# A second layer norm and expert router moved from their own stage into a tile pipeline of attention

## The reference

```python
a   = layer_norm(c, ln1_w, ln1_b); a = conv1d(a, conv_w)          # causal, 3 taps
q, k, v = split(a @ attn_w); q, k = rotary(q), rotary(k)
y   = softmax(causal(q @ k.T / sqrt(16))) @ v                       # 16 heads of 16, sequences of 64
s   = c + y @ proj_w
h   = layer_norm(s, ln2_w, ln2_b)                                   # the second norm
idx = argmax(h @ router_w)                                          # 4 experts, the first of equals
out = x1 + s + sum_e where(idx == e, swiglu_e(h), 0)                # x1: the output of the first block
```

## Time and profile before

| | us |
|---|---|
| median of three runs | 2254.34 (2252.97 to 2255.35) |
| the profiled execution, its own time | 2255.13 |
| span of its profile | 2253.3 |
| tile pipeline, first TensorE work to last add | 1876.75 to 1975.19 |
| `layer_norm` stage, to the first matmul of the sort | 1976.07 to 2017.59 |
| first matmul of the experts | 2040.73 |

### The profile page before, as it was taken

How to read it: one execution, slowest core, us unless ns; L and a number is a source line. 1 busy time by engine, 2 the same in 40 slices (tenths; PEclk the granted TensorE clock), 3 DMA queues, 4 the chain that set the end, 5 groups by cost and what they waited for, 6 DMA issues and landing times. The chain is left out here.

```text
span 2253.3 us, 32388 instructions
## 1 busy us (share of the span) xinstructions
PE 2053.0 (91%) x11764; PEld 1725.6 (77%) x11764; DVE 1120.4 (50%) x1969; ACT 941.9 (42%) x1879; POOL 666.2 (30%) x713
## 2 busy tenths in 40 slices
PE   7999999999999999999998666899899666868998
PEld 6888888888888888888886455688799455747998
DVE  3333443434344344434435785423477566756775
ACT  4242323323232332424224697322355354555664
POOL 3030200203030120303100396110388143308884
PEclk9999999999999999999999698899899878978999
DMA  4010010101001010200001200410156123246661
GB/s 160 1 57 1 1 56 0 56 0 56 0 11 45 0 56 0 81 0 0 1 1 38 53 36 31 149 38 10 53 198 195 41 44 109 78 142 206 212 215 57
DMA packets 93436, 139.98 MB, mean 62 GB/s; under 512 B 15438, under 2 KB 70384, under 8 KB 93360
## 3 DMA queue, kind: packets, MB, share of 16 engines
q1 hardware_dynamic: 86304, 122.97, 17.1%
q0 software_dynamic: 4928, 12.86, 1.6%
q10 hardware_dynamic: 2128, 3.15, 0.4%
HBM read 106.96 MB, written 12.06 MB: 53 GB/s over the span
## 5 line engine op out<-in xcount | busy, mean ns | idle before, releaser
L584 DVE TENSOR_TENSOR cond_h<-cond_silu,ps 128x512 f32<-128x512 f32 x288 | 197.9, 687 | 697.6 <-ACT cond_silu L495 694.1
L495 ACT ACTIVATE cond_silu<-ps 128x512 f32<-128x512 f32 x288 | 172.3, 598 | 772.6 <-PE ps L414 772.6
L414 PE MATMUL ps<-a_x_hi,cond_w_hi 128*128 128x512 f32 x1152 | 449.8, 390 | 2.0 <-DVE a_x_lo L262 2.0
L414 PE MATMUL ps<-a_x_lo,cond_w_hi 128*128 128x512 f32 x1152 | 449.3, 390 | 0.0
L414 PE MATMUL ps<-a_x_hi,cond_w_lo 128*128 128x512 f32 x1152 | 449.1, 390 | 0.0
L383 POOL TENSOR_TENSOR cond_w_lo<-cond_stage_up,cond_w_hi 128x256 fp32r<-128x256 f32 x144 | 108.6, 771 | 833.7 <-ACT cond_w_hi L476 833.7
L414 PEld LDWEIGHTS ps<-a_x_hi,cond_w_hi 128*128 128x128 f32 x1152 | 216.9, 188 | 47.5 <-DVE a_x_lo L262 2.4
L414 PEld LDWEIGHTS ps<-a_x_hi,cond_w_lo 128*128 128x128 f32 x1152 | 216.9, 188 | 45.3
L414 PEld LDWEIGHTS ps<-a_x_lo,cond_w_hi 128*128 128x128 f32 x1152 | 216.9, 188 | 45.0
L430 PE MATMUL ps<-cond_h_hi,cond_d_hi 128*128 128x512 f32 x576 | 224.4, 390 | 3.4 <-DVE cond_h_lo L552 3.4
L430 PE MATMUL ps<-cond_h_hi,cond_d_lo 128*128 128x512 f32 x576 | 224.1, 389 | 0.0
(11 more groups left out here) (371 smaller groups left out, 4086.4 us busy)
## 6 DMA issues: line engine op xcount, KB each, us to landing
moe_stage_up<-in_L_ffn_expert_wv SPq DMA_DIRECT2D x22, 1024.0 KB, 8.4
typed_stage_up<-in_L_cond_wi SPq DMA_DIRECT2D x11, 1024.0 KB, 4.9
typed_stage_dn<-in_L_cond_wo SPq DMA_DIRECT2D x11, 1024.0 KB
moe_stage_dn<-in_L_ffn_expert_proj SPq DMA_DIRECT2D x11, 1024.0 KB
cond_stage_up<-in_L_cond_Wg SPq DMA_DIRECT2D x7, 1024.0 KB, 4.8
cond_stage_up<-in_L_cond_Wu SPq DMA_DIRECT2D x7, 1024.0 KB, 6.8
cond_stage_dn<-in_L_cond_Wd SPq DMA_DIRECT2D x7, 1024.0 KB, 5.1
hyp_v_now<-hyp_v_blk SPq DMA_DIRECT2D x16, 272.0 KB, 2.3
```

Of the source, the lines that this page charges most:

```text
L414: ins = pe.matmul(up_ps[st % 2][j], w[:, j, k, fs], x[:, k, tok], start=(i == 0), stop=(i == 3 * KC - 1))
L495: act.activation(silu[:, st % 2], up_ps[st % 2][0], ACT.Silu).then_inc(act_done, 1)
L584: dve.tensor_tensor(h[:, st % 2], silu[:, st % 2], up_ps[st % 2][1], ALU.mult).then_inc(up_free, 1)
```

## The change

`layer_norm` and its block are gone. The tile pipeline of the rotary attention has ten further phases, with tokens on the partitions:

- `out` now multiplies so that tokens are on the partitions (two matmuls 256 columns wide), and adds c by two matmuls of `router.res` (that tile's chunk of `m.sumT`, copied by SyncE) with the identity into the same bank. `add` is gone.
- `bring_sum` (SyncE, lag 4): two DMAs per tile, `router.res`, and `router.x` (the tile's rows of x1, from `typed_table` in HBM, where they already are).
- `stats`, `aggr` (VectorE), `rstd` (ScalarE, two small activations), `norm`, `total` (VectorE, read `out`'s bank), `weigh` (GpSimd, times ln2_w and plus ln2_b, rows), `store` (SyncE, one DMA per tile of h and total rows into `moe_table`).
- `h_turn` (TensorE, lag 6), `h_take` (ScalarE), `route` (TensorE), `keep` (VectorE, copies the logits). After the last tile `choose` picks the experts for all tiles at once, in nine small VectorE instructions.
- `y_take`, `out` have lag 5 instead of 4, the last lag is 6 instead of 4.
- hT_ps shares bank 0 with q's transposes, the logits bank 1 with k's, and y's transposes share bank 7 with `out`, which `norm` and `total` read; the added waits keep them apart.
- The weights of slot 0 are loaded at the head of the sort block (`SortFirst.sync`).

```diff
-            lag = dict(bring=0, turn=1, q_blk=1, k_blk=1, score=1, clamp=2, top=2, shift=2, prob=2, p_turn=3, p_take=3,
-                       mix=3, y=3, y_turn=4, y_take=4, out=4, add=4, fetch=1)
-            order = dict(tensor="y_turn p_turn out turn mix score", scalar="y_take p_take q_blk prob",
-                         vector="clamp top add k_blk y", gpsimd="shift", sync="bring fetch")
+            lag = dict(bring=0, turn=1, q_blk=1, k_blk=1, score=1, clamp=2, top=2, shift=2, prob=2, p_turn=3, p_take=3,
+                       mix=3, y=3, y_turn=4, y_take=5, out=5, fetch=1, bring_sum=4, stats=5, aggr=5, rstd=5, norm=5, total=5,
+                       weigh=5, h_turn=6, h_take=6, route=6, keep=6, store=6)
+            order = dict(tensor="out p_turn h_turn turn mix score route y_turn",
+                         scalar="y_take p_take h_take q_blk rstd prob",
+                         vector="clamp top stats k_blk aggr y norm total keep", gpsimd="shift weigh",
+                         sync="bring fetch bring_sum store")
...
+                    def bring_sum(i, q, nth):
+
+                        wait(sp, out_done, i - 1)
+                        sp.dma_start(router.res[:, q], resT[:, :, bass.ds(i * P, P)]).then_inc(sum_brought[q], 16)
+                        wait(sp, added, i - 1)
+                        sp.dma_start(router.x[:, q], router.x_rows[bass.ds(i * P, P)]).then_inc(sum_brought[q], 16)
+
+                    def store(i, q, nth):
+
+                        sp.wait_ge(weighed, i + 1)
+                        sp.wait_ge(added, i + 1)
+                        sp.dma_start(router.table[bass.ds(i * P, P)], router.rows[:, q]).then_inc(stored[q], 16)
+
+                    if not hyper:
+                        router.load(sp)
...
                         wait(pe, k_blocked, i)
+                        if not hyper:
+                            wait(pe, kept, i - 5)
...
                         wait(pe, q_taken, i)
+                        if not hyper:
+                            wait(pe, h_taken, i - 4)
...
                         wait(pe, y_taken, i)
                         wait(pe, added, i)
+                        if not hyper:
+                            wait(pe, normed, i)
...
                     def out(i, q, nth):
                         pe.wait_ge(y_taken, i + 1)
                         wait(pe, added, i)
+                        if not hyper:
+                            wait(pe, normed, i)
+                            pe.wait_ge(sum_brought[q], 32 * (nth + 1))
+                            for k in range(KC):
+                                pe.matmul(o_ps, yT[:, q, k], wo[:, k], start=(k == 0), stop=False)
+                            for c in range(KC):
+                                ins = pe.matmul(o_ps[:, c * P:(c + 1) * P], router.res[:, q, c], m.ident, start=False, stop=(c == KC - 1))
+                            ins.then_inc(out_done, 1)
+                            return
...
+                    def total(i, q, nth):
+
+                        dve.wait_ge(sum_brought[q], 32 * (nth + 1))
+                        wait(dve, stored[q], 16 * nth)
+                        dve.tensor_tensor(router.rows[:, q, D:], o_ps, router.x[:, q], ALU.add).then_inc(added, 1)
...
+                    def weigh(i, q, nth):
+
+                        pool.wait_ge(normed, i + 1)
+                        wait(pool, stored[q], 16 * nth)
+                        wait(pool, h_turned, i - 1)
+                        pool.tensor_tensor(router.xn[:, q], router.xn[:, q], router.w[:], ALU.mult).then_inc(scaled, 1)
+                        pool.wait_ge(scaled, i + 1)
+                        pool.tensor_tensor(router.rows[:, q, 0:D], router.xn[:, q], router.b[:], ALU.add).then_inc(weighed, 1)
...
     def sync(self, sp):
+        self.slots.load_slot(sp, 0, 0)
         sp.wait_ge(self.lists.owned, 1)
```

More of the change, by code:

```diff
@@ L1062, in bring @@
                         sp.dma_start(x[:, q], qk[:, bass.ds(i, 1)].rearrange("p o n -> p (o n)")).then_inc(brought[q], 16)
-                    run(sp, "sync", dict(bring=bring, fetch=fetch))
+                    def bring_sum(i, q, nth):
[9 more added lines that the diff above has]
+                        router.load(sp)
+                    run(sp, "sync", dict(bring=bring, fetch=fetch, bring_sum=bring_sum, store=store))
                 @block.tensor
@@ L1141, in out, with h_turn, route @@
                         ins.then_inc(out_done, 1)
-                    run(pe, "tensor", dict(turn=turn, score=score, p_turn=p_turn, mix=mix, y_turn=y_turn, out=out))
+                    def h_turn(i, q, nth):
+                        pe.wait_ge(weighed, i + 1)
+                        wait(pe, h_taken, i)
+                        wait(pe, q_taken, i + 5 if not isinstance(i, int) else min(i + 5, NP))
+                        for c in range(KC):
+                            ins = pe.transpose(hT_ps[:, c * P:(c + 1) * P], router.rows[:, q, c * P:(c + 1) * P], m.ident)
+                        ins.then_inc(h_turned, 1)
+                    def route(i, q, nth):
+                        pe.wait_ge(h_taken, i + 1)
+                        wait(pe, kept, i)
+                        wait(pe, k_blocked, i + 6 if not isinstance(i, int) else min(i + 6, NP))
+                        for c in range(KC):
+                            ins = pe.matmul(lg_ps, router.hT[:, q, c], router.wr[:, c], start=(c == 0), stop=(c == KC - 1))
+                        ins.then_inc(routed, 1)
+                    if not hyper:
+                        pe.wait_ge(router.loaded, 16 * len(router.loads))
+                    run(pe, "tensor", dict(turn=turn, score=score, p_turn=p_turn, mix=mix, y_turn=y_turn, out=out, h_turn=h_turn, route=route))
                 @block.scalar
@@ L1206, in block_k @@
                         wait(dve, scored, i - 1)
+                        if not hyper and not isinstance(i, int):
+                            dve.wait_ge(gathered, i + 1 + lag["k_blk"] - lag["stats"])
                         shape = [P, KC * 2, GH, T]
@@ new lines, in add, with statistics, aggregate @@
+                        ins.then_inc(added, 1)
+                    def statistics(i, q, nth):
+                        dve.wait_ge(out_done, i + 1)
+                        wait(dve, rstd_done, i - 1)
+                        dve.bn_stats(router.stats[:, q], o_ps).then_inc(gathered, 1)
+                    def aggregate(i, q, nth):
+                        if isinstance(i, int):
+                            dve.wait_ge(gathered, i + 1)
+                        dve.bn_aggr(router.mean[:, q], router.stats[:, q]).then_inc(averaged, 1)
@@ new lines, in keep @@
+                    def keep(i, q, nth):
+                        dve.wait_ge(routed, i + 1)
+                        dve.tensor_copy(router.logits[:, bass.ds(i, 1)].rearrange("p o e -> p (o e)"), lg_ps).then_inc(kept, 1)
+                    phases = dict(stretch=stretch, k_blk=block_k, clamp=clamp, top=top, y=scale_y, add=add)
+                    if not hyper:
+                        phases = dict(k_blk=block_k, clamp=clamp, top=top, y=scale_y, stats=statistics, aggr=aggregate, norm=normalize, total=total, keep=keep)
@@ L1253, in _ @@
+                    run(dve, "vector", phases)
+                    if not hyper:
+                        dve.wait_ge(kept, NP)
+                        router.choose(dve, chosen)
                 @block.gpsimd
@@ L1268, in shift @@
                                            ALU.subtract).then_inc(shifted, 1)
-                    run(pool, "gpsimd", dict(root_add=root_add, mask=mask, shift=shift))
+                    def weigh(i, q, nth):
[5 more added lines that the diff above has]
+                        pool.tensor_tensor(router.rows[:, q, 0:D], router.xn[:, q], router.b[:], ALU.add).then_inc(weighed, 1)
+                    if not hyper:
+                        pool.memset(router.eps[:], LN_EPS).then_inc(eps_set, 1)
+                        pool.wait_ge(router.loaded, 16 * len(router.loads))
+                    run(pool, "gpsimd", dict(root_add=root_add, mask=mask, shift=shift, weigh=weigh))
         sem.give_back()
@@ L1943, in scalar @@
     def scalar(self, act):
[L1944 removed]
+        self.wait_stored(act)
     def vector(self, dve):
@@ L2324, in program @@
         m.typed_rows = scratch("typed_rows", N, D)
+        moe_stored = [ctx.enter_context(nc.semaphore(f"moe_stored{q}")) for q in range(2)]
         m.slot_expert = sb("slot_expert", [P, SLOTS], I32)
@@ L2405, in program @@
             brief.close()
-            attention(nc, m, "rope", False, s0, m.sumT, rope)
+            second.close()
+            router = Router(nc, s, a["L0_ffn_ln2_w"], a["L0_ffn_ln2_b"], a["L0_ffn_router_w"], typed_table, moe_table, m.moe_sel)
+            attention(nc, m, "rope", False, s0, m.sumT, rope, router, moe_stored)
         with ExitStack() as s:
```

261 lines of the change are left out of this document (76 added, 185 removed).

## The result

The changed kernel takes 2298.43 us (median of 4 runs, 2297.42 to 2299.50) against 2254.85 for the kernel before beside it: ratio 1.0190, 95% interval 1.0172 to 1.0208. That is 43.6 us slower; the forecast was 26.3 (2281), and 2298.4 lies at the very top of its range of 2263 to 2298. The sign and the chain of waits came out as forecast, the clock did not.

A forecast was written before the change was run, and what follows sets the result against it. It took TensorE to bound the tile pipeline before, and waits on SyncE's DMAs after. 2255.1 + 22.3 (later sort) + 1 (slot 0's weights) + 3 (clock) = 2281.4, less 0.8 for the median: 2281 us, range 2263 to 2298.

The forecast's parts named there:

- 11 full steps: Tile loop with all router phases: eleven steps of 9.16 us each, 5.47 to the end of `mix` plus 3.69.
- the clock term: TensorE in the loop: one of eleven steps at 1.2 GHz instead of full clock, costing 3 us.
- the DMA path: From `mix` to the next `out` through SyncE's bring_sum loads, issued behind fetch: 3.69 us, setting the step at 9.16.
- the computing path: From `mix` to the next `out` through y, norm, total and y's transposes: 2.89 us, alone giving 8.36 a tile.
- Slot 0's load: Slot 0's weights, now loaded at the sort's head: between nothing and 4 us, taken as 1.
- The DMAs did not land in time: Rival for the loop: bring_sum's loads land in time, 8.36 us a tile, 2270 us; chance 0.22.
- TensorE was not the bound: Rival for the loop: TensorE stays the bound, 6.7 us a tile, 2243 us, faster than before; chance 0.08.
- The clock falls: Rival for the loop: half of the eleven steps at 1.2 GHz, costing 18 us instead of 3, 2296 us; chance 0.15.
- a clock under 0.8 in the loop: Profile sign of the rival in which TensorE's clock falls: granted clock under 0.8 in the tile loop.
- the point of decision: Step time in the loop from which TensorE staying the bound would be decided: 7.5 us a tile.

The follow-up runs named there:

- e1_sync: Kernel after the change with SyncE's row as bring, bring_sum, fetch, store, so the loads for `out` no longer queue behind fetch; 2266.27 us.
- e2_hturn: Kernel after the change with h_turn heading TensorE's row, ahead of `out`, and h_take ahead of p_take on ScalarE; 2295.25 us.
- e9_fill_out: Kernel after the change with ten unread transposes added behind y_turn, in TensorE's wait ahead of `out`; 2284.96 us.
- e6_h_mid: Kernel after the change with bring_sum ahead of fetch on SyncE, h_turn between `out` and p_turn, and h_take ahead of p_take; 2267.13 us.
- e3_both: Kernel after the change with bring_sum ahead of fetch on SyncE, h_turn heading TensorE's row, and h_take ahead of p_take; 2271.22 us.
- e4_fill: Kernel after the change with unread transposes added: ten behind y_turn and six between k's and q's transposes; 2283.24 us.
- e7_ring: Kernel after the change with SyncE, TensorE, ScalarE and VectorE rows reordered together, route behind y_turn, keep a step later; 2247.23 us, 0.9958 of the kernel before.

## Why the prediction was right in sign and short in size

The stage, step by step, in us (the second column is the prediction's working):

| part of the stage | forecast | measured | off by |
|---|---|---|---|
| first issue to first transposes, beyond the 2.4 of before | 1.5 | 2.0 | +0.5 |
| first transposes to `out` of tile 0 | 22.7 | 22.6 | -0.1 |
| `out` of tile 0 to tile 1 | 8.6 | 9.9 | +1.3 |
| 11 full steps | 100.8 | 119.1 | **+18.3** |
| `out` of tile 12 to tile 15 | 20.3 | 22.8 | +2.5 |
| `out` of tile 15 to the sort | 9.4 | 12.0 | +2.6 |

Together 25.1, which with the forecast 22.3 are the 47.4 that the stage grew by. (The time grew by less, as the sort was 0.8 shorter and the stage began 2.7 sooner in that execution.)

**The step that failed is the clock term**, "Between none and all eleven I take one: 3". Its size was taken from the first attention, which is busy 66% at full clock. The runs show that the busy share does not decide: e1_sync holds 1.00 at 77% while e2_hturn has 0.84 at the same share, and e9_fill_out holds 1.00 at 79% with e6_h_mid and e3_both below it at 80 and 78%. A difference that the rows did show is in the waits. The first attention of the kernel before has three in a step, 1.3 us at the longest, in 1300 to 1340:

```profile
PE ps L1106 <- ACT hyp_prob L1178: 7.7, 6, 1.3
PE ps L1119 <- ACT hyp_pT L1183: 3.7, 5, 0.9
PE ps L1139 <- ACT hyp_yT L1188: 2.1, 5, 0.5
```

The change has one of 1.5 to 2.3 in every step, and filling that one brought the clock back (e9_fill_out). I should have set the waits that my own path gave (0.8 us between the DMA path and the computing path, on top of the wait for yT) beside those of the first attention, and not the shares. That would have been a warning and not a number: with waits that are alike, nine of the eleven steps lost the clock and two kept it.

The term came to 15.7 us in the 11 steps. The first step, from `out` of tile 0 to that of tile 1, adds 1.4 (9.87 at a mean clock of 0.83; 8.44 in e4_fill at 1.00). It may also have made part of the 5.1 of drain and tail: `out` of tile 15 takes 2.07 in place of 1.13, for instance. That part was not tested, as e4_fill and e9_fill_out did not raise the clock in the tail.

The term was wrong twice, in opposite directions. One step was counted and nine lost the clock; such a step was priced at 3.3 us, and it cost 1.7 (15.7 / 9), as the clock was low in part of it only. The prediction had weighed a kernel that the Trainium skill tells of (TensorE: Matmul & The Clock Gate, HAM oscillation), whose TensorE waits 3 to 5 us for a DMA in every tile and falls to half clock each time. The trace here agrees in kind and not in every step: the waits for the DMA were shorter, 1.5 to 2.3 us, and the clock fell to half in nine steps of eleven.

**The paths were right.** `out` to `mix` was 4.27 and `mix` 1.13, together 5.40 for 5.47. `mix` to `out` by SyncE was 3.89 (2001.43 to 2005.32) for 3.69; the issue of router_x was 1.69 behind `mix` there and not 1.39 (each issue follows the one before by 0.71 and 0.85, not 0.63), and the landing 2.2, for 2.3 taken. e1_sync and e4_fill agree with both: 8.2 on average without the DMA path (8.36 forecast) and 9.4 with it. Of the parts, `norm` was put too low: VectorE takes 0.54 for it, not 0.42 at most.

**Slot 0's load cost nothing.** The sort took 22.3 us to the experts' first matmul (2062.27 to 2084.56), 23.1 before; moe_stage_up landed in 9.2 and GpSimd needed it 17.5 us into the sort. The term of 1 was within its bounds.

**The rivals.** The DMAs did not land in time, and TensorE was not the bound. "The clock falls", at 0.15 and 2296 us, is the one that came about in size (2298.4), though its sign, a clock under 0.8 in the loop, was missed narrowly: 0.81 to 0.83. That its 18 us are near the 15.7 is luck in part: half of the steps at 3.3 us each, where nine lost 1.7 each. The rival on the other side took its 6.7 us a tile from work queued ahead in the waits; e7_ring shows the way it could have gone, with 7.0 a tile and 2247. It passes the point of decision that the prediction gave, 7.5. (The chances of a slower kernel add up to 0.87 there, not 0.88.)

## What to carry to other kernels

A DMA that feeds the next step should not be queued behind one that waits for this step's last result: swapping two words in the queue's order was worth 32 us of 44. When a change opens waits on TensorE, read the granted clock step by step and not the busy share alone, and fill the longest wait with unread work as a test: the waits of some 1.7 us for a transfer came with another 1.4 us a step in lost clock. And before a fused stage is given up as slower, walk its ring once and move each engine's work to where that engine waits anyway.

## What was not expected of the hardware

Added work made the kernel faster: ten unread transposes in a wait of 1.7 us took 13.5 us off (2298.43 to 2284.96), while six in a wait of 1.0 us took nothing off (2302.80). The clock was also low (0.84) in e2_hturn, where no single wait is over 1.1 us but two stand close together; in e1_sync, with waits of 1.0 and 0.8 that lie apart, it was 1.00. That their closeness is the cause is a guess that no run tested. What exactly lets the clock fall stays open here: the kernel after the change keeps it in two steps of eleven with the same waits, e3_both and e6_h_mid lose it in a few steps of an otherwise regular loop, and no view shows how those steps differ from their neighbours.
